# Alternating the rows of two products that share a stationary block, in the first eight of an iteration's 44 rows

## The reference, cut to what matters

```
x = x + ffn0(cond0(x))      # per-sample 64x64 mix, then the low-rank product A @ B.T, plus bias
x = x + ffn1(cond1(x))      # grouped 9-tap convolution along the features plus context,
                            # then W_up (1024 x 1024) and a top-1 choice of four rank-8 experts
...
base_out = jnp.einsum('bth,oh->bto', x, W_up)
```

## Time and profile before

| | |
|---|---|
| runs | 1100.01, 1100.12 and 1095.28 us; median 1100.01 |
| profiled execution | span from first to last instruction 1092.4 us; no separate time of this execution is given, and the median stands 7.6 us above the span |
| TensorE matmuls busy | 1070.1 us (98%), 7034 matmuls, 7034 weight loads |
| VectorE busy | 905.4 us (83%) |
| ScalarE busy | 604.3 us (55%) |
| chain that ended last | 93% TensorE, 3% VectorE, 2% DMA |
| granted TensorE clock, mean over the span | 0.995 of full |

### The profile page before, as it was taken

How to read it: one execution, slowest core, us unless ns; L and a number is a source line. 1 busy time by engine, 2 the same in 40 slices (tenths; PEclk the granted TensorE clock), 3 DMA queues, 4 the chain that set the end, 5 groups by cost and what they waited for, 6 DMA issues and landing times.

```text
span 1092.4 us, 19196 instructions
## 1 busy us (share of the span) xinstructions
PE 1070.1 (98%) x7034; PEld 1033.6 (95%) x7034; DVE 905.4 (83%) x1663; ACT 604.3 (55%) x1233; POOL 5.8 (1%) x22
## 2 busy tenths in 40 slices
PE   6799999999999999999999999999999999999998
PEld 5689999999999999999999999999999999999998
DVE  7998888888888888888888888888888888888774
ACT  6775556555556555556555556555556555555441
POOL 1000000000000000000000000000000000000000
PEclk9899999999999999999999999999999999999999
DMA  9945544445544445544545544455554445544412
GB/s 343 289 118 154 155 131 119 116 139 156 152 134 118 118 141 154 153 133 118 115 144 154 147 138 119 116 143 154 140 146 117 113 145 156 146 139 96 83 59 78
DMA packets 123340, 152.71 MB, mean 140 GB/s; under 512 B 26384, under 2 KB 96528, under 8 KB 122992
## 3 DMA queue, kind: packets, MB, share of 16 engines
q1 hardware_dynamic: 121360, 149.12, 49.7%
q10 hardware_dynamic: 1888, 2.38, 0.7%
HBM read 81.29 MB, written 36.21 MB: 108 GB/s over the span
## 4 chain that ended last, share of the span: by engine, by line
PE 93%; DVE 3%; DMA 2%; SPq 1%; issue 0%; ACT 0%; ACTq 0%; DVEq 0%
PE M L1537 45%; PE F L1486 8%; PE H L1537 8%; PE F L1436 8%; PE G L1537 7%; PE F L1407 2%; PE F L1406 2%; PE F L1408 2%; PE M L1572 2%; PE M L1460 2%; PE G L1460 2%; DMA agb_scratch<-small 1%; PE F L1424 1%; PE F L1423 1%; SPq L390 0%
## 5 line engine op out<-in xcount | busy, mean ns | idle before, releaser
L1537 PE MATMUL M<-Wsh,yh 128*128 128x412 f32 x896 | 322.1, 359 | 0.1
L1537 PE MATMUL M<-Wsh,yl 128*128 128x412 f32 x896 | 313.3, 350 | 0.0
L1537 PE MATMUL M<-Wsl,yh 128*128 128x412 f32 x896 | 313.1, 349 | 0.0
L1006 DVE STREAM_TRANSPOSE yr<-F 128x512 f32<-128x512 f32 x126 | 90.1, 716 | 103.6 <-PE F L1486 103.4
L1537 PEld LDWEIGHTS M<-Wsh,yh 128*128 128x128 f32 x896 | 169.0, 189 | 3.9 <-DVE x L1137 0.6
L1537 PEld LDWEIGHTS M<-Wsl,yh 128*128 128x128 f32 x896 | 169.1, 189 | 2.9
L1537 PEld LDWEIGHTS M<-Wsh,yl 128*128 128x128 f32 x896 | 168.2, 188 | 0.9
L503 ACT ACTIVATE yh<-yr 128x1024 fp32r<-128x1024 f32 (+1 forms) x127 | 120.1, 947 | 22.5 <-DVE yr L1021 16.6
L617 ACT ACTIVATE F<-G,cbs 128x128 f32<-128x128 f32 x248 | 69.3, 342 | 70.3 <-PE G L1460 70.3
L617 ACT ACTIVATE F<-M,cbs 128x128 f32<-128x128 f32 x248 | 69.3, 343 | 59.2 <-PE M L1460 59.2
L503 ACT ACTIVATE F<-biasb 128x512 f32<-128x512 f32 x124 | 74.4, 601 | 44.4 <-DVE yr L1006 43.3
(11 more groups left out here) (236 smaller groups left out, 2474.4 us busy)
## 6 DMA issues: line engine op xcount, KB each, us to landing
x<-in_xP_dram SPq DMA_DIRECT2D x64, 516.0 KB, 4.2
xTr<-in_xT_dram SPq DMA_DIRECT2D x64, 512.0 KB, 3.8
Xr<-x SPq DMA_DIRECT2D x502, 64.5 KB, 2.5
out_dram<-x SPq DMA_DIRECT2D x62, 516.0 KB, 3.1
agb<-agb_scratch SPq DMA_DIRECT2D x31, 128.0 KB, 3.3
agg_scratch<-stage SPq DMA_DIRECT2D x2, 1024.0 KB, 6.2
agg<-agg_scratch SPq DMA_DIRECT2D x60, 32.0 KB, 3.4
Wsr<-in_Wsd_dram ACTq DMA_DIRECT2D x2, 824.0 KB, 8.2
```

The lines of the kernel that those rows point to most:

```text
L1006: dve.transpose(dst.rearrange("p j k m -> p (j k) m").rearrange("p (k r) (g b n) -> p g b k r n", r=2, g=2, b=4)[:, g % 2], F[g % 2][:, :] ...
L1537: last = pe.matmul(dst, w[:, y, k, :], m, start=fresh and n_ == 0, stop=k == 3 and n_ == 2, skip_group_check=True)
```

## The change

In the loop over `it`, the first eight rows of an iteration are issued in another order. Before: rows 0, 1, 2, 3 of block 0, and then rows 0, 1, 2, 3 of block 1. After: row 0 of block 0, row 0 of block 1, row 1 of block 0, row 1 of block 1, and so on. The waits stay with their rows, and no other engine's list is touched. Iteration 0 is written out apart and stays as it was.

```diff
                 for n in range(44):
                     b = n // 4
-                    if late and 12 <= n < 20:
+                    if n < 8:
+                        row(it, n % 2, n // 2)
+                    elif late and 12 <= n < 20:
 
                         row(it, 3 if 14 <= n < 18 else 4, n - 14 if 14 <= n < 18 else n - 12 if n < 14 else n - 16)
                     else:
```

## The result

| | before | after |
|---|---|---|
| median of the runs | 1099.2 us (4 runs, 1095.3 to 1100.1) | 1138.0 us (4 runs, 1137.6 to 1139.2) |
| ratio | | 1.037, 95% interval 1.035 to 1.0389 |
| span of the profiled execution | 1092.4 us | 1136.2 us |
| distance between iterations, 2 to 29 | 32.79 us | 34.22 us |

The changed kernel is slower, by 3.7% in the ratio of the runs (the two medians alone stand 3.5% apart). All distances between iterations in this document are taken in one way: the start of ScalarE's copy H<-G in iteration 29 less that in iteration 2, divided by 27.

A forecast was written before the change was run, and what follows sets the result against it. TensorE, busy 98% of the span, was taken as the bound. Waits of 0.61 + 0.15 + 0.60 + 0.04 us in 28 iterations, plus iterations 1, 30 and 31, gave 43.1 us: 1143 us, range 1130 to 1156.

The forecast's parts named there:

- First wait, `f12`: Block 1's first weight load comes early and waits for VectorE's addition; 0.61 us lost per steady iteration.
- Second wait, copy G to H: Block 0 ends late, so block 2 waits for ScalarE's copy; 0.15 us lost per steady iteration.
- Third wait, copy A to B: Block 3 waits for ScalarE's copy, queued behind two rounding copies and the delayed G to H; 0.60 us per steady iteration.
- The chain that is late next: VectorE's line 974 starts 1.39 us late, and the router's chain of 3.27 us before the transpose follows.
- the extra 0.04 us at the transpose: Transpose's load goes 0.16 us late behind the router's chain; 0.07 free, 0.05 paid before, 0.04 us more lost.
- The alternation at 0: Switching between narrow and wide matmuls costs nothing itself; bounds -1 and +2 us over the run.
- The sum: 1.39 us in 28 iterations, 38.9; plus 1.8 in iteration 1 and 2.4 in iterations 30 and 31: 43.1 us.
- Between the span and the median of the runs stand 7.6 us: Gap between profiled span and median time, assumed to stay 7.6 us when forecasting the changed kernel's time.
- Only two waits binding: Rival, chance 0.10: ScalarE reaches copy A to B in time; 25 us lost, 1125 us.
- Spreading: Rival, chance 0.13: ScalarE needs 0.24 us more and VectorE's chain reaches the transpose another 0.16 late; 54 us, 1154 us.
- The clock: Rival, chance 0.03: TensorE's short pauses lower its clock for a tenth of each iteration; 53 us more, 1196 us.
- Stationary block kept: Rival, chance 0.04: neighbouring rows' equal stationary block stays in the array, freeing time; no loss or a gain, 1100 or 1087 us.

The follow-up runs named there:

- e1: Kernel before with only row 0 of block 1 moved early, behind one row of block 0; distance 33.43 us, ratio 1.0174 to the kernel before.
- e2: Kernel before with the last row of block 0 moved behind three rows of block 1; distance 33.64 us, ratio 1.0208 to the kernel before.
- e3: Kernel before with the last row of block 0 moved behind row 0 of block 1; distance 32.84 us, ratio 1.0019 to the kernel before.
- e4: Changed kernel with ScalarE's two rounding copies moved ahead of copy G to H, iteration 30 excepted; distance 33.63 us, ratio 1.0236 to the kernel before.
- e9: Changed kernel with the transpose one row later, behind row 17 but ahead of unit_v; distance 34.22 us, ratio 1.0395 to the kernel before.
- e10: Kernel before with the transpose one row later, behind row 17 but ahead of unit_v; distance 32.83 us, ratio 1.0003 to the kernel before.
- e11: Kernel before, unchanged, profiled again in one execution; distance 32.83 us, span 1095.3 us, no ratio taken.
- e12: Changed kernel, unchanged, run and profiled again; distance 34.22 us, ratio 1.0387 to the kernel before.
- e5: Changed kernel with ScalarE's rounding copies moved behind both bank copies, in all iterations; distance 34.91 us, ratio 1.0562 to the kernel before.
- e6: Changed kernel with the transpose one row later, behind row 17 and unit_v; distance 34.34 us, ratio 1.040 to the kernel before.

## Why the prediction was right, and where it wasn't

**First wait, `f12`: right.** 0.61 forecast, 0.62 read, and 0.60 by itself in e1 (over 32.83). The load stood until 0.05 us after the addition's end in all 31 iterations; none passed its wait. e2 and e3, which give it three narrow rows of cover back, are without it in all but three iterations.

**Second wait, copy G to H: right in kind, too small.** 0.15 forecast, 0.21 read. The mis-sized step is how long a copy's end takes to reach a load. The prediction took the 0.05 us of VectorE's addition for ScalarE's copy as well. The copy H<-G ended at 538.39 and the load went at 538.50, the copy M<-M at 540.32 and its load at 540.43: 0.11 us each time. The third wait has the same 0.06 in it, but block 2 is late by as much, so it doesn't show in that term.

**Third wait, copy A to B: right.** 0.60 forecast, 0.59 read. The choice of 1.79 us from iteration 1 over the 2.04 of iteration 14 decides 0.24 us an iteration; the changed kernel took 1.78. e4 shows that the queue ahead of the copy makes this wait, since moving that queue removes it.

**The chain that is late next: its lateness right, its cost wrong.** Line 974 started at 5.75 (5.77 forecast). But the extra 0.04 us at the transpose isn't there. Its load stood at 543.28, 0.05 behind the chain's end (543.04 plus 0.19), and its matmul at 543.34 is still one wide pitch behind the one in front (543.15). Block 3 is late by 1.38 already, against 1.39 for the whole iteration, and moving the transpose out of the way in e9 and e10 changed nothing. The two errors, 0.06 too little and 0.04 too much, nearly cancel. That the forecast's 1.39 us is the measured 1.39 to the last digit is therefore in part luck; the terms themselves are good to 0.06.

**The alternation at 0: right.** e3 against e11 is 0.01 us, with two of the six additional changes; within the full alternation the pitches are the old ones (under the rivals below).

**The sum.** 43.1 us were forecast on the span and 43.8 measured (1136.2 less 1092.4), of which 28 x 1.43 = 40.0 in the steady iterations (28 x 0.04 = 1.1 of it owed to the first profile, not to the change), 0.4 before the loop (the first copy H<-G at 57.10 against 56.68), and the rest, 3.4, in iterations 1, 30 and 31. There 4.2 was forecast. Iteration 1 is the one that was mis-sized, 1.4 us against 1.8: the load of its block 2 already had 0.35 us of idle time in front of it, waiting for VectorE's line 1056, before the change, which the sum left out. The medians rose by 38.8 us in the first runs (1099.2 to 1138.0) and by 42.7 in e12 (1098.5 to 1141.2) (the time before the loop alone differs by some us between executions, see the last section). The forecast of 1143 us missed the measured 1138.0 by 5 because of another step: "Between the span and the median of the runs stand 7.6 us, taken as unchanged". In the thirteen profiled executions whose time is also known (the changed kernel's and those of e1 to e12), 1.7 to 1.8 us stand between the two (1136.2 and 1137.92 in the changed kernel). By that the first profile was of an execution of about 1094 us, shorter than any of the four timed ones (1095.3 to 1100.1), and the rest of the 7.6 was the distance from it to their median. From its span the forecast would have been 1135.5 + 1.7 = 1137.2.

**The rivals.** Only two waits binding: refuted by the wait for copy M<-M in 29 iterations. Spreading: refuted by the distance, though e5 shows that it lies one copy away. The clock: 0.995 in both, with pauses of 0.2 to 0.6 us in all iterations. The rule of the Trainium skill ("TensorE: Matmul & The Clock Gate", "A second HAM failure mode: psum-queue depth-cycling"), by which frequent short idles between groups of matmuls make the clock oscillate, did not act on pauses of this size. Stationary block kept: refuted, every row in the alternating stretch has its 3 loads, and its pitch is the old one (e.g. 537.51 to 537.84 for a narrow row).

## What to carry to other kernels

Before rows are reordered, look for two things at each row: which wait stands on it and how many rows were its cover, and whose copy starts at its end and how many rows stand between that end and the copy's consumer. Alternating two accumulations brings the start of one forward and pushes the end of the other back, and both uncover waits even where the matmuls themselves cost the same. An engine at 55% busy can hold the kernel up if its fixed order puts other work between two copies; ask what is queued ahead of each copy once it comes late.

## What was not expected of the hardware

The time before the loop varies between executions of one and the same stretch of code. The first copy H<-G stood between 56.7 and 61.7 us in the traces of this study, and it moved the whole span with it, while the distance between iterations differed by 0.04 us at most between traces of one kernel. In the two traces of the changed kernel (57.10 and 61.60) most of the difference comes from TensorE's rate: 0.45 us at 17.3 us, it is 4.95 at 30.8. The same eight weight loads of line 1589 in the first of them and in e12:

```profile
19.31 0.97 PEld L1589 LDWEIGHTS F<-onesr,Bh 128*128 128x128 f32 x8
```

```profile
21.28 1.83 PEld L1589 LDWEIGHTS F<-onesr,Bh 128*128 128x128 f32 x8
```

In e12 TensorE works at about half the rate from 17 to 28.8 us; in the first trace it does so only from 22.9 to 26.3 in that part, and the view of stretches gives a granted clock of 0.50 there (24 to 26 us), the lower of the two levels. For e12 the view gives 1.00 in the same part, although its loads of lines 1406 to 1408 stand 0.21 us apart as they do at 0.50 in the other trace. So a granted clock near 1 in the record isn't proof of the full rate; the distance between like matmuls is. Why the slow part is longer in some executions was not tried. Where a change acts in each iteration, the distance from one trace decides finer than the ratio of the times does.

From the recorded end of a ScalarE copy to the start of the weight load that waited for it were 0.11 us, from that of VectorE's addition 0.05 us. In the changed kernel it was 0.11 for the copy H<-G in all 31 iterations, 0.11 for the copy M<-M in 29, and 0.05 for the addition in all 31. The copy zst of e6 has 0.11 or 0.12 too.
